# Handing out expert slots in blocks of 128 rows instead of tiles of 256, with up products 128 columns wide

## What is computed

```python
logits = einsum('bsd,de->bse', x, Wg)                 # x: layer-normed, 4096 tokens, E = 8 experts
top_vals, top_idx = top_k(logits, 2)                  # two experts a token
probs = softmax(top_vals)                             # their shares
for e in range(E):
    u = x @ W1[e]; v = x @ W2[e]                      # 256 -> 512, the up products
    h = u * sigmoid(u) * v
    y = h @ W3[e]                                     # 512 -> 256, the down product
    out = out + y * weights[..., e][..., None]
```

## Time and profile before

| | us |
|---|---|
| median of 3 runs | 1856.62 |
| the profiled execution | 1860.18 |
| its span, first to last instruction | 1858.5 |
| first load of `e` to the last one (39 tiles) | 694.3 to 1023.3 |
| last scatter of the stage starts | 1037.9 |

### The profile page before, as it was taken

How to read it: one execution, slowest core, us unless ns; L and a number is a source line. 1 busy time by engine, 2 the same in 40 slices (tenths; PEclk the granted TensorE clock), 3 DMA queues, 4 the chain that set the end, 5 groups by cost and what they waited for, 6 DMA issues and landing times. The chain is left out here.

```text
span 1858.5 us, 33579 instructions
## 1 busy us (share of the span) xinstructions
PE 1334.2 (72%) x12235; PEld 1026.7 (55%) x12235; DVE 1092.5 (59%) x1991; ACT 759.4 (41%) x1278; POOL 734.9 (40%) x628
## 2 busy tenths in 40 slices
PE   3777648788773329999999277844788872299997
PEld 1555425566652218888888277522556542256665
DVE  4777645777665655555555562374777746744443
ACT  1222335656545643433334140132576671234433
POOL 1110147989873363444444110061577893000000
PEclk9787768788765559999999655555887875599999
DMA  3000066654514421222122520007523210000000
GB/s 138 1 0 0 18 135 110 111 95 70 86 19 139 158 80 56 60 64 64 58 64 58 201 107 2 0 0 149 123 53 70 53 19 0 1 12 12 23 23 23
DMA packets 83949, 114.07 MB, mean 61 GB/s; under 512 B 11620, under 2 KB 68070, under 8 KB 81384
## 3 DMA queue, kind: packets, MB, share of 16 engines
q1 hardware_dynamic: 76328, 91.78, 21.6%
q0 software_dynamic: 7488, 20.46, 3.7%
HBM read 72.98 MB, written 31.20 MB: 56 GB/s over the span
## 5 line engine op out<-in xcount | busy, mean ns | idle before, releaser
L2756 POOL TENSOR_TENSOR q_pl<-q_ex,q_ph 128x512 f16<-128x512 f32 x128 | 147.0, 1161 | 44.4 <-ACT q_ph L2710 44.0
L1776 POOL TENSOR_TENSOR r_siml<-r_sim,r_simh 128x512 f16<-128x512 f32 x128 | 146.2, 1161 | 21.3 <-ACT r_simh L1680 20.9
L1089 POOL DMA_INDIRECT expert_results<-mt_yout,m_deliver x78 | 77.4, 993 | 171.4 <-ACT mt_yout L1177 159.4
L2559 DVE TENSOR_REDUCE q_mx<-q_pS 128x4 f32<-128x512 f32 x128 | 86.5, 685 | 76.1 <-PE q_pS L2487 75.5
L1538 DVE TENSOR_TENSOR r_sim<-r_pS,r_causal 128x512 f32<-128x512 f32 x128 | 86.5, 682 | 60.3 <-PE r_pS L1452 56.5
L1122 PE MATMUL mt_pU<-mt_xh,m_w 128*128 128x256 f16 x624 | 116.2, 274 | 1.5 <-DVE mt_xl L1198 1.5
L1680 ACT ACTIVATE r_simh<-r_sim 128x512 f16<-128x512 f32 x128 | 79.9, 628 | 90.2 <-DVE r_sim L1538 85.6
L1122 PE MATMUL mt_pV<-mt_xh,m_w 128*128 128x256 f16 x624 | 115.2, 273 | 0.0
L1133 PE MATMUL mt_pY<-m_w,mt_hh 128*128 x624 | 106.5, 272 | 10.8 <-DVE mt_hl L1212 10.7
L2704 ACT ACTIVATE q_ex<-q_pE 128x512 f32<-128x512 f32 x128 | 76.6, 599 | 67.4 <-PE q_pE L2508 44.3
L2978 DVE TENSOR_TENSOR s_hc<-s_h,s_pC 128x512 f32<-128x512 f32 x64 | 44.0, 688 | 100.8 <-ACT s_h L2947 100.8
(11 more groups left out here) (503 smaller groups left out, 4144.3 us busy)
## 6 DMA issues: line engine op xcount, KB each, us to landing
ahead<-in_L_ffn_W SPq DMA_DIRECT2D x12, 1024.0 KB, 5.0
r_kstack<-k_bounce SPq DMA_DIRECT2D x48, 128.0 KB, 4.7
r_qstack<-q_bounce SPq DMA_DIRECT2D x48, 128.0 KB, 5.9
q_Q<-m_bounce SPq DMA_DIRECT2D x24, 256.0 KB
X<-in_x SPq DMA_DIRECT2D x4, 1024.0 KB, 7.9
r_ctx<-in_ctxT SPq DMA_DIRECT2D x8, 512.0 KB, 5.6
k_bounce<-r_ksplit SPq DMA_DIRECT2D x32, 128.0 KB, 2.6
q_bounce<-r_qsplit SPq DMA_DIRECT2D x32, 128.0 KB, 2.4
```

The source lines that it names most:

```text
L1089: pool.indirect_dma_start(results[:, :], bass.IndirectOffsetOnAxis(ap=deliver[:, at:at + 1], axis=0), yout[n % 2][:, a, :], None).then_inc ...
L1776: pool.tensor_tensor(siml[n % RING][:, :], sim[n % SIMS][:, :], simh[n % RING][:, :], ALU.subtract)\
L2559: dve.tensor_reduce(mx[:, at:at + UNIT], pS[n % 2][:, :, :], AX, ALU.max).then_inc(s["taken"], 1)
L2756: pool.tensor_tensor(pl[n % RING][:, :], ex[n % 3][:, :], ph[n % RING][:, :], ALU.subtract)\
```

## The change

A slot block becomes the unit: TILE = 128, so that `TILES` = 72 blocks (71 would hold any split, rounded up to an even number) and each block has an owner. `PAIRS` = 36 pairs of blocks take the place of the 39 tiles in `expert_tiles`; a pair still has 256 rows in all buffers, but its two blocks may belong to two experts. `up` therefore issues its matmuls for each block apart, 128 columns wide. Two scratch tiles of `dispatch` become fp16.

```diff
-TILE = 2 * P
-TILES = (2 * B * S + E * (TILE - 1)) // TILE
+TILE = P
+PAIRS = -(-((2 * B * S + E * (TILE - 1)) // TILE) // 2)
+TILES = 2 * PAIRS
 STEPS = B * S // TILE
-BLOCKS = TILES * TILE // P
+BLOCKS = TILES
...
-    more, ahead_of = r.sb("more", [P, E, STEPS]), r.sb("ahead_of", [P, E, E])
+    more, ahead_of = r.sb("more", [P, E, STEPS], f16), r.sb("ahead_of", [P, E, E])
...
-    passed, owner_f = r.sb("passed", [P, TILES, E - 1]), r.sb("owner_f", [P, TILES])
+    passed, owner_f = r.sb("passed", [P, TILES, E - 1], f16), r.sb("owner_f", [P, TILES])
...
-            def up(n, p, half, e, first):
+            def up(n, p, half, owners, first):
...
                     for j in range(HALF):
                         cols = slice((half * HALF + j) * P, (half * HALF + j + 1) * P)
-                        for m, (dc, x, y) in enumerate(steps):
-                            last = pe.matmul(ps[half][:, j, :], W[x][:, e, dc, cols], (xh, xl)[y][p][:, dc, :],
-                                             start=(m == 0), stop=(m == len(steps) - 1))
+                        for a, e in enumerate(owners):
+                            rows_of = slice(a * P, (a + 1) * P)
+                            for m, (dc, x, y) in enumerate(steps):
+                                last = pe.matmul(ps[half][:, j, rows_of], W[x][:, e, dc, cols],
+                                                 (xh, xl)[y][p][:, dc, rows_of],
+                                                 start=(m == 0), stop=(m == len(steps) - 1))
                     last.then_inc(sem, 1)
...
-            def down(n, half, e, first):
+            def down(n, half, owners, first):
...
-                    for a in range(BLK):
+                    for a, e in enumerate(owners):
...
-            for n in range(TILES):
-                e = pe.value_load(owner[0:1, n:n + 1], min_val=0, max_val=E - 1)
-                up(n, n % 2, 0, e, n == 0)
+            for n in range(PAIRS):
+                owners = [pe.value_load(owner[0:1, n * BLK + a:n * BLK + a + 1], min_val=0, max_val=E - 1)
+                          for a in range(BLK)]
+                up(n, n % 2, 0, owners, n == 0)
```

More of the change, by code:

```diff
@@ L1053, in expert_tiles @@
     HALF = HC // 2
-    BLK = TILE // P
+    BLK = 2
+    WIDE = BLK * TILE
     INPUTS = 4
-    turn = c.ps("turn", [P, DC, TILE])
-    pU, pV = ([c.ps(f"{n}{i}", [P, HALF, TILE]) for i in range(2)] for n in ("pU", "pV"))
+    turn = c.ps("turn", [P, DC, WIDE])
+    pU, pV = ([c.ps(f"{n}{i}", [P, HALF, WIDE]) for i in range(2)] for n in ("pU", "pV"))
     pY = c.ps("pY", [P, BLK, D])
@@ L1060, in expert_tiles @@
     yout = [c.sb(f"yout{i}", [P, BLK, D]) for i in range(2)]
-    xh, xl = ([c.sb(f"{n}{i}", [P, DC, TILE], f16) for i in range(2)] for n in ("xh", "xl"))
-    sg, t_, h = ([area[:, (2 * n + i) * HALF * TILE:(2 * n + i + 1) * HALF * TILE].rearrange(
+    xh, xl = ([c.sb(f"{n}{i}", [P, DC, WIDE], f16) for i in range(2)] for n in ("xh", "xl"))
+    sg, t_, h = ([area[:, (2 * n + i) * HALF * WIDE:(2 * n + i + 1) * HALF * WIDE].rearrange(
         "p (a t) -> p a t", a=HALF) for i in range(2)] for n in range(3))
-    hh, hl = ([c.sb(f"{n}{i}", [P, HALF, TILE], f16) for i in range(2)] for n in ("hh", "hl"))
+    hh, hl = ([c.sb(f"{n}{i}", [P, HALF, WIDE], f16) for i in range(2)] for n in ("hh", "hl"))
     loaded = [c.sem(f"loaded{i}") for i in range(INPUTS)]
@@ L1093, in _ @@
                 gather(n)
-            for n in range(TILES):
+            for n in range(PAIRS):
                 scatter(n)
-                if n + INPUTS < TILES:
+                if n + INPUTS < PAIRS:
                     gather(n + INPUTS)
             for i in range(2):
-                pool.wait_ge(stored[i], 16 * BLK * len(range(i, TILES, 2)))
+                pool.wait_ge(stored[i], 16 * BLK * len(range(i, PAIRS, 2)))
         @block.tensor
@@ L1140, in _ @@
             before = None
-            for n in range(TILES):
-                e = pe.value_load(owner[0:1, n:n + 1], min_val=0, max_val=E - 1)
-                up(n, n % 2, 0, e, n == 0)
+            for n in range(PAIRS):
+                owners = [pe.value_load(owner[0:1, n * BLK + a:n * BLK + a + 1], min_val=0, max_val=E - 1)
+                          for a in range(BLK)]
+                up(n, n % 2, 0, owners, n == 0)
                 if n > 0:
                     down(n - 1, 1, before, False)
-                if n + 1 < TILES:
+                if n + 1 < PAIRS:
                     transpose(n + 1)
[L1148 to L1151, removed]
+                up(n, n % 2, 1, owners, n == 0)
+                down(n, 0, owners, n == 0)
+                before = owners
+            down(PAIRS - 1, 1, before, False)
         @block.scalar
@@ L1183, in step @@
                     result(n - 1, k - 1 + p, 1 - p, not starts(n, 1) and not starts(n, 2))
-                if not starts(n, TILES - 1):
+                if not starts(n, PAIRS - 1):
                     high(n + 1, 1 - p, age > 0)
@@ L1189, in _ @@
             high(0, 0, False)
-            for n in range(TILES):
+            for n in range(PAIRS):
                 step(n, n // 2, n % 2, min(n, 2))
-            result(TILES - 1, (TILES - 1) // 2, 0, True)
+            result(PAIRS - 1, (PAIRS - 1) // 2, (PAIRS - 1) % 2, True)
         @block.vector
```

## The result

The changed kernel takes 1937.28 us (median of 4 runs, 1936.55 to 1938.27); beside it the kernel before took 1855.92 us (1853.77 to 1857.04). The ratio is 1.044 (95% interval 1.0422 to 1.0458): slower, by 81.4 us. The forecast was 1929 us in a range of 1905 to 1957.

A forecast was written before the change was run, and what follows sets the result against it. TensorE's array sets the pace before, its sequencer after, at 11.4 us a pair. +70 (35 periods), +3 (last pair), -0.6 (dispatch) make +72 on 1860.2, so 1932; less 3.6 to the median: 1929 us, range 1905 to 1957.

The forecast's parts named there:

- What bounds it: Expert stage: TensorE's array sets the pace before the change, its sequencer's register instructions after it.
- Part 1, fewer passes: Expert loop: 36 pairs for 39 tiles, three periods of 8.66 us fewer, 26 us if nothing else changed.
- part 2, the array's 8.45 us: Array's work in a pair: up 5.4 us for 5.24, with down 2.62 and transposes 0.44.
- Part 3, 11.4 us a pair: Sequencer's work in a pair: up 7.7 us, down 1.9, owner loads 1.3, waits 0.5; +70 us over 35 periods.
- The period as a sum: Expert loop: a pair's period is the sum of the sequencer's own instructions, 11.4 us, over the array's 8.45.
- The waits of the earlier trace: Down's waits for `hl` before the change: absorbed by the slower sequencer, 14 us already contained in the forecast.
- Last pair +3: Last pair, load to last matmul: longer by one owner load (0.65 us) and two up halves (3.85 for 2.62).
- dispatch -0.6: Dispatch before the expert stage: smaller `in_block` work, larger `passed`; stage starts about 0.6 us earlier, bounds -1.5 to +1.
- the step to the median: Whole kernel: 3.6 us taken off 1932, as the profiled execution stood that much above the median; gives 1929.
- A: Rival, sequencer: addresses stay hidden, an address costing under 0.12 us; 8.8 us a pair, -21, 1836 us; 6%.
- B: Rival, up's matmuls: weight loads set the pace, at worst 109 ns a matmul, +144, 2003 us; 5% for over 0.09 us.
- C: Rival, TensorE clock: holes in up lower it, 16.2 us a pair, +238 + 3, about 2097 us; 4%.

The follow-up runs named there:

- experiments 1 and 2: Changed kernel with both blocks using the first's owner, loaded once: 1821.68 us, ratio 0.9865; with experts as program constants, no owner loads: 1825.75 us, ratio 0.9886.
- experiment 11: Changed kernel without the owners' range checks, its gathers and scatters as plain transfers issued by SP instead of GpSimd's indirect ones: 1902.09 us, ratio 1.0241.
- experiment 9: Changed kernel with a pair's two owner loads, range checks kept, moved half a pair earlier, behind the transposes: 1953.17 us, ratio 1.0515.
- experiment 12: Kernel before with gathers and scatters as plain transfers issued by SP instead of GpSimd's indirect ones: 1838.15 us, ratio 0.9897.
- experiment 3: Kernel before with each tile's owner loaded into two registers that the matmuls use by turns, matmuls still 256 wide: 1899.66 us, ratio 1.0293.
- before_again: Kernel before, unchanged, run and profiled once more on another chip: 1857.99 us, ratio 0.9999.
- experiment 4: Changed kernel with a sequencer branch in each half of up, taking wide matmuls where both blocks have one owner: 1847.61 us, ratio 1.0016.

## Why the prediction was right

- **What bounds it.** Right. The sequencer is the bound: experiments 1 to 3 move the time with the number of addresses, and of the loads of owners that come with them, while the matmuls stay as they are.
- **Part 1, fewer passes; part 2, the array's 8.45 us.** Right: 8.42 to 8.46 us in experiments 1 and 2, where three tiles fewer give 1.1 to 1.4%. The earlier trace rows has four such matmuls in a row; the same trace has runs of eight, with starts 55 to 56 ns apart as well:

```profile
1307.08 0.61 PE L2487 MATMUL q_pS<-q_KM,q_Q 128*128 128x128 f16 x8
```

- **Part 3, 11.4 us a pair.** 11.585 measured. The mis-sized term is the address: 0.12 us taken, 0.1225 measured over whole pairs (80 x 0.0025 = 0.2 us a pair, 7 us in all). A free-running half of 15 intervals in rows rounded to 0.1 us couldn't tell these apart; a window over several halves would have. The two owner loads at 1.3 us stand: from the first load to the second it is 0.65 us, and the period without both checks is 0.57 us shorter (experiment 11 against the changed kernel).
- **The period as a sum.** It holds for the changed kernel, whose trace has hardly a stop. That is luck: the forecast didn't know of the stops, and with the same instructions in another order they cost 17 us (experiment 9). Why the order matters is open.
- **The waits of the earlier trace rows.** That they would be absorbed was right. Their cause was misread: the text laid them to the chain sigmoid, t, h, hh, hl, which is under 4 us and not late by itself; it starts late because `u_done` or `v_done` arrives late (experiment 12: with no late update the waits are gone). The "remote" line in the list of waits said so, and wasn't taken up.
- **Last pair +3, dispatch -0.6.** Measured +2.1 and -1.0. `passed` in fp16 output took 0.67 us, as estimated. POOL's two pieces again end late, 18.42 us from 656.45 where the two of 633.38 took 8.13: by the reckoning of part 4 the first was let go at 666.7 us, while `passed` ran (666.27 to 666.94).
- **The 8 us between 1929 and 1937.3.** Half is the sum: +76.3 us measured between the profiled executions for +72, of which the period has +6.5. The other half is the step to the median: 3.6 us were taken off because the execution profiled before stood that much above its median, and the one profiled after stood 0.7 under its own.
- **Rivals.** A falls to the even 0.12 us. B falls to experiments 1 and 2: 56 ns a matmul through 48 in a row, none over 57; at anything up to (11.4 - 3.06) / 96 = 87 ns the sequencer's 11.4 us would still have ended last. The part of B that the forecast's range takes in is an estimate that no run shows. C falls to the clock of 1.00; its 213 ns is what 256 columns took at the stage's start, at a granted clock of 0.50 from 694 to 698 us.

## What to carry to other kernels

The busy share said nothing about the sequencer: PE was busy 37.11 of 40 us in a stage whose pace the register instructions set. Where addresses come from a register, count the distinct ones between two waits, times the 0.12 us measured here, and hold that against the matmuls beside them. Halving a matmul's columns halved the time that hides its address, from 109 to 56 ns. And when a wait's releaser is "remote", as for 89.7 us in the changed kernel, look also at what another engine issues at that moment, not only at the chain that waits.

## What the runs showed of the hardware

- **Register instructions.** On record for 32 and 46 ns, they cost 0.1125 to 0.124 us from start to start, 0.1225 in the mean, with a longer interval of 0.14 to 0.3 us about every eighth, also with GpSimd idle (experiment 11). What these longer intervals are isn't shown. A load of a register takes 0.36 us until the next instruction, its range check 0.29 more; in experiment 3 the first of two loads took some 0.56.
- **Indirect transfers and semaphores.** A `v_done` over 1 us late came 3.1 us late in the changed kernel and 1.6 in the one before (medians), and "remote" waits stood in the stage on every chip but one where GpSimd issued the transfers. On that one (experiments 1 to 4) no `v_done` was late and the kernel before took 1843.8 us. The gathers' own record differs too: the first row is of `before_again`, the second of `before_two_registers` on that chip.

```profile
L1081 POOL DMA_INDIRECT mt_xin<-token_rows,m_fetch x78: 942/962/1270, 686.3 to 1006.5; - x78
```

```profile
L1081 POOL DMA_INDIRECT mt_xin<-token_rows,m_fetch x78: 942/990/1282, 688.2 to 1044.7; - x78
```

- **A branch** on TensorE's sequencer takes 0.38 us in the median until the next instruction (0.13 to 0.63, experiment 4).
- **Open.** Why one chip is free of the late updates; what the changed kernel would take there; whether it is the indirect kind, the issuing engine or the rows' order that holds the updates; whether spacing GpSimd's transfers out, or issuing them while TensorE loads its owners, gives the 11.7 us back with the look-up in place. None of these was tried.
